# FC1 in 128 channels and two side-by-side halves of 64, and FC2's bias on POOL, in a shifted-window attention block

## The reference, cut to what matters

```python
f = residual + f.transpose(0, 3, 1, 2)
m = _ln(f.transpose(0, 2, 3, 1), g2, b2)
m = jax.nn.gelu(m @ w_fc1 + b_fc1, approximate=False) @ w_fc2 + b_fc2
return f + m.transpose(0, 3, 1, 2)
```

## Time and profile before

| | us |
|---|---|
| median of 3 runs (2 others: 3062.35, 3064.25) | 3063.34 |
| the profiled execution | 3062.91 |
| its span, first to last instruction | 3061.1 |
| TensorE busy (matmuls) | 2862.6 |
| VectorE, ScalarE, POOL busy | 2424.3, 2076.6, 1454.5 |

### The profile page before, as it was taken

How to read it: one execution, slowest core, us unless ns; L and a number is a source line. 1 busy time by engine, 2 the same in 40 slices (tenths; PEclk the granted TensorE clock), 3 DMA queues, 4 the chain that set the end, 5 groups by cost and what they waited for, 6 DMA issues and landing times.

```text
span 3061.1 us, 137479 instructions
## 1 busy us (share of the span) xinstructions
PE 2862.6 (94%) x53060; PEld 2299.2 (75%) x53060; DVE 2424.3 (79%) x7208; ACT 2076.6 (68%) x3208; POOL 1454.5 (48%) x1832
## 2 busy tenths in 40 slices
PE   1799999999999999999999999999999999999997
PEld 0677777777777777777777777777777777777775
DVE  5778888788887888788787888878888788888885
ACT  0467767667776767767766767767767667777674
POOL 2554454454444444444444454444454454445444
PEclk9899999999999999999999999999999999999999
DMA  1444444444444444444444444444444444444441
GB/s 29 108 119 123 124 125 119 119 126 122 126 127 113 123 123 122 126 121 120 124 126 114 125 124 120 124 123 120 123 125 118 120 126 121 126 127 119 125 113 42
DMA packets 414727, 359.37 MB, mean 117 GB/s; under 512 B 63455, under 2 KB 413985, under 8 KB 414012
## 3 DMA queue, kind: packets, MB, share of 16 engines
q1 hardware_dynamic: 414028, 350.01, 43.7%
HBM read 193.25 MB, written 154.14 MB: 113 GB/s over the span
## 4 chain that ended last, share of the span: by engine, by line
PE 87%; issue 5%; ACT 5%; DVE 2%; POOL 1%; SPq 0%; DMA 0%; POOLq 0%; DVEq 0%; ACTq 0%
PE psum L446 18%; PE psum L379 16%; PE psum L559 11%; PE psum L430 10%; PE psum L414 8%; PE psum L472 7%; PE psum L487 6%; PE psum L532 5%; ACT probs L618 4%; PE psum L522 3%; PE psum L395 2%; PE psum L511 1%; DVE st L754 1%; POOL rs L349 0%; DVE xfl L765 0%
## 5 line engine op out<-in xcount | busy, mean ns | idle before, releaser
L618 ACT ACTIVATE probs<-psum 113x784 f32<-113x784 f32 x768 | 633.2, 824 | 652.0 <-PE psum L430 648.9
L730 DVE TENSOR_REDUCE nmax<-psum 113x16 f32<-113x784 f32 x768 | 745.3, 970 | 153.9 <-PE psum L414 153.3
L342 POOL TENSOR_SCALAR ve<-mv 98x8 f32<-98x8 f32 x264 | 64.5, 244 | 1482.4 <-DVE mv L759 1476.5
L446 PE MATMUL psum<-vbd,probs 128*49 128x18 f32 x24576 | 644.2, 198 | 9.8 <-issue 9.0
L446 PEld LDWEIGHTS psum<-vbd,probs 128*49 128x49 f32 x24576 | 634.4, 126 | 14.1 <-issue 13.3
L349 POOL TENSOR_TENSOR rs<-ve,half 98x8 f32<-98x8 f32 x264 | 440.0, 1667 | 0.0
L430 PE MATMUL psum<-qbd,kst 128*49 128x196 f16 x6144 | 405.1, 251 | 36.3 <-DVE xfl L765 23.2
L754 DVE BATCH_NORM_STATS2 st<-tok 98x6 f32<-98x96 f32 x2112 | 363.6, 245 | 84.3 <-ACT tok L625 70.8
L354 POOL TENSOR_TENSOR xn<-xn,rs 98x768 f32<-98x768 f32 x264 | 388.4, 1471 | 72.7 <-POOL rs L349 72.7
L414 PE MATMUL psum<-kbd,qst 128*49 128x196 f16 x6144 | 401.4, 250 | 7.6 <-issue 4.2
L765 DVE TENSOR_TENSOR xfl<-psum,xfh 96x784 f16<-96x784 f32 x264 | 256.0, 970 | 176.0 <-ACT xfh L630 174.2
(11 more groups left out here) (83 smaller groups left out, 5270.1 us busy)
## 6 DMA issues: line engine op xcount, KB each, us to landing
stack_pages<-nat SPq DMA_DIRECT2D x256, 294.0 KB, 3.0
kst<-stack_pages SPq DMA_DIRECT2D x256, 220.5 KB
qbd<-stack_pages SPq DMA_DIRECT2D x1024, 55.1 KB
stack_pages<-nat SPq DMA_DIRECT2D x256, 147.0 KB, 2.0
xr<-in_x_dram SPq DMA_DIRECT2D x224, 147.0 KB, 3.4
out_dram<-yr SPq DMA_DIRECT2D x224, 147.0 KB, 2.2
qst<-stack_pages SPq DMA_DIRECT2D x256, 73.5 KB
kbd<-stack_pages SPq DMA_DIRECT2D x1024, 18.4 KB
```

Of the source, the lines that this page charges most:

```text
L446: last = nc.tensor.matmul(dst[:, :, h, :], probs[:, b.c % 2, h // 4, p, h % 4 * L:(h % 4 + 1) * L], vbd[:, b.c % 4, p * NH + h, :, :], sta ...
L618: nc.scalar.activation(probs[0:PR, b.c % 2, u, :, :].rearrange("j (g q) k -> j g (q k)", g=2), psum[0:PR, B:B + 2, 0:2 * CH], ACT.Exp).the ...
L730: nc.vector.tensor_reduce(dst, psum[0:PR, A:A + 2, 0:2 * CH].rearrange("i g (q h j) -> i g q h j", q=2, j=L), axis=AX.X, op=ALU.max, negat ...
```

## The change

FC1 now makes hidden channels 0 to 127 for all 392 tokens of a band with one group of three matmuls on the whole array (`most_and_rest`, first loop), written as two pieces of 196 tokens into the two halves of one bank. The remaining 64 channels (`REST`) are made for tokens 0 to 195 on partitions 0 to 63 and for tokens 196 to 391 on partitions 64 to 127 of the next bank, in turn, three pairs of matmuls over 196 columns. The Gelu reads these three pieces, 3 x 196 elements on 128 partitions, and `hid` has that shape. FC2 works on half a band (196 tokens) at a time: the first 128 hidden channels with `w2[:, 0]`, and the third piece with weights that are zero for the other half's 64 partitions (`w2[:, 1 + s]`). There is no free partition for the row of ones, so POOL adds FC2's bias to f before VectorE adds FC2 to it, with a semaphore `f_biased` that `result` waits for.

```diff
+PART = TOK // 2
+REST = HID - 128
+BIAS = -4
...
-        wp, w2 = sb("wp", [FULL, C]), sb("w2", [FULL, 2, C])
-        vec = sb("vec", [C, 5])
+        wp, w2 = sb("wp", [FULL, C]), sb("w2", [FULL, 3, C])
+        vec = sb("vec", [C, 6])
...
-        hid = sb("hid", [FULL, 2, 2, TOK])
+        hid = sb("hid", [FULL, 2, 3, PART])
...
+        def three_parts(bank):
+            return psum[:, bank:bank + 2, :].rearrange("p b (s r) -> p (b s) r", s=2)[:, 0:3, 0:PART]
...
+            const(w2[:, 0, :], wfc2[0:FULL, :])
             for m in range(2):
-                const(w2[0:C, m, :], wfc2[m * C:(m + 1) * C, :])
-            const(w2[C:C + 1, 0, :], bfc2.rearrange("(a c) -> a c", a=1))
+                const(w2[REST * m:REST * (m + 1), 1 + m, :], wfc2[FULL:HID, :])
...
+            def add_bias(b):
+                pool.wait_ge(t_made, b.step(AFTER).count(1, 1))
+                alone(pool)
+                nc.gpsimd.tensor_scalar(f[:, b.c % 8, :], f[:, b.c % 8, :], vec[:, BF:BF + 1], None, ALU.add).then_inc(f_biased, 1)
...
                 if has(t.step(ORDER)):
                     order_x(t.step(ORDER))
+                if has(t.step(BIAS)):
+                    add_bias(t.step(BIAS))
...
+            def most_and_rest(bank, high, low, b, kind):
+                products = ((high, xfh), (high, xfl), (low, xfh))
+                for n, (weights, tokens) in enumerate(products):
+                    nc.tensor.matmul(three_parts(bank)[:, 0:2, :], weights[:, 0:FULL], tokens[:, b.c % 4, kind, :].rearrange("c (s t) -> c s t", s=2),
+                                     start=n == 0, stop=n == 2)
+                for n, (weights, tokens) in enumerate(products):
+                    for s in range(2):
+                        last = nc.tensor.matmul(psum[REST * s:REST * (s + 1), bank + 1, 0:PART], weights[:, FULL:FULL + REST], tokens[:, b.c % 4, kind, s * PART:(s + 1) * PART],
+                                                start=n == 0, stop=n == 2)
+                return last
...
-                for m in range(2):
-                    last = three(psum[0:C, (B, A)[n] + m, 0:TOK], w1h[:, m * C:(m + 1) * C], w1l[:, m * C:(m + 1) * C], b, 1)
+                last = most_and_rest((B, A)[n], w1h, w1l, b, 1)
...
-                for m in range(2):
-                    last = nc.tensor.matmul(psum[0:C, D + n, 0:TOK], w2[:, m, :], hid[:, b.c % 2, m, :], start=m == 0, stop=m == 1)
+                for s in range(2):
+                    dst = psum[0:C, D + n, s * PART:(s + 1) * PART]
+                    nc.tensor.matmul(dst, w2[:, 0, :], hid[:, b.c % 2, s, :], start=True, stop=False)
+                    last = nc.tensor.matmul(dst, w2[:, 1 + s, :], hid[:, b.c % 2, 2, :], start=False, stop=True)
...
-                nc.scalar.activation(hid[0:C, b.c % 2, :, :], psum[0:C, at:at + 2, 0:TOK], ACT.Gelu, scale=1 / GAIN).then_inc(gelu_done, 1)
+                nc.scalar.activation(hid[:, b.c % 2, :, :], three_parts(at), ACT.Gelu, scale=1 / GAIN).then_inc(gelu_done, 1)
...
-            for a in (wide, wide1, wp, w2, xfh, xfl, oT, hid, kst, probs):
+            nc.vector.memset(w2[:, 1:3, :], 0.0)
+            for a in (wide, wide1, wp, xfh, xfl, oT, kst, probs):
...
-            nc.vector.memset(hid[C:C + 1, :, 0, :], 1.0).then_inc(rows_one, 1)
...
                 dve.wait_ge(fc2_made, b.count(1, 1))
+                dve.wait_ge(f_biased, b.count(1, 1))
```

More of the change, by code:

```diff
@@ L62 @@
 AFTER = 8
+BIAS = -4
 HIDDEN, RESULT, STORE = (-5, -4), (-6, -5), (-7, -6)
-N_CONST = 9 + 5 + 4 + 6
+N_CONST = 9 + 6 + 4 + 6
 class Band:
@@ L115, in build @@
         w1h, w1l = sb("w1h", [FULL, HID], F16), sb("w1l", [FULL, HID], F16)
-        wp, w2 = sb("wp", [FULL, C]), sb("w2", [FULL, 2, C])
-        vec = sb("vec", [C, 5])
-        G1, B1, BP, G2, B2 = range(5)
+        wp, w2 = sb("wp", [FULL, C]), sb("w2", [FULL, 3, C])
+        vec = sb("vec", [C, 6])
+        G1, B1, BP, G2, B2, BF = range(6)
         xr = sb("xr", [C, 4, WS, SIDE])
@@ L175, in build @@
         ot_made, o_in, proj_made, f_made = sem("ot_made"), sem("o_in"), sem("proj_made"), sem("f_made")
+        f_biased = sem("f_biased")
         fc1_made, gelu_done, fc2_made, y_made = sem("fc1_made"), sem("gelu_done"), sem("fc2_made"), sem("y_made")
@@ L229, in _ @@
             const(wp[0:C, :], wproj)
+            const(w2[:, 0, :], wfc2[0:FULL, :])
             for m in range(2):
-                const(w2[0:C, m, :], wfc2[m * C:(m + 1) * C, :])
-            const(w2[C:C + 1, 0, :], bfc2.rearrange("(a c) -> a c", a=1))
+                const(w2[REST * m:REST * (m + 1), 1 + m, :], wfc2[FULL:HID, :])
             const(brow[C:C + 1, :], bqkv.rearrange("(a c) -> a c", a=1))
             const(brow1[C:C + 1, :], bfc1.rearrange("(a c) -> a c", a=1))
-            for n, v in ((G1, g1), (B1, b1), (BP, bproj), (G2, g2), (B2, b2)):
+            for n, v in ((G1, g1), (B1, b1), (BP, bproj), (G2, g2), (B2, b2), (BF, bfc2)):
                 column(n, v)
@@ L701, in _ @@
             dve.wait_ge(filled, 1)
-            nc.vector.memset(xfh[C:C + 1, :, :, :], 1.0)
-            nc.vector.memset(hid[C:C + 1, :, 0, :], 1.0).then_inc(rows_one, 1)
+            nc.vector.memset(xfh[C:C + 1, :, :, :], 1.0).then_inc(rows_one, 1)
             nc.vector.memset(psum[:, :, :], 1.0).then_inc(psum_clear, 1)
```

## The result

The changed kernel took 3044.98 us (median of four runs, 3039.4 to 3049.6), the kernel before 3062.85 beside it: a ratio of 0.9942, 95% interval 0.9922 to 0.9963. It is faster, by 17.9 us and not by 42. In a second set of runs it was 0.9931 (0.9914 to 0.9948). The forecast of 3021 and the range from 3000 to 3034 were wrong.

A forecast was written before the change was run, and what follows sets the result against it. TensorE, busy 94% of the span, was taken as the bound, waiting for the second Gelu ahead of the transposes. From 3062.9 us, 128 x 0.34 = 43.5 saved, FC2 +3 and start -1 gave 3021; range 3000 to 3034.

The forecast's parts named there:

- The steady pair: One ordinary pair of steps: transposes start 0.34 us sooner, FC2 costs 0.024 more, pairs 0.32 us shorter.
- the switches: FC1 on TensorE: changing between whole array and halves costs 0.12 us in and 0.10 out, 0.34 in FC1.
- the halves: FC1's 64-channel matmuls over 196 columns run side by side: 0.085 us a pair, six pairs 0.51.
- rival 1: FC1's halves don't run side by side at 64 channels: FC1 2.34 us, kernel 3084 us; chance 0.06.
- rival 4: Gelu on ScalarE keeps its 0.82 us: only 0.18 us a pair, 23 us, kernel 3042; chance 0.06.
- rival 3: TensorE's mode changes in FC1 cost nothing: 0.50 us a pair sooner, 64 us, kernel 3001; chance 0.08.
- rival 2: Weight loads of short matmuls lie open: in FC2 up to +1.31 us a pair, kernel 3187; chance 0.03.
- about 0.3: Sign expected in the changed profile: TensorE's wait ahead of the transposes, 0.47 us before, at about 0.3.
- 3010: Fast end of the forecast's own range, 3010 to 3032, taken from a gain of 0.45 us a pair.
- POOL's add: FC2's bias added on POOL once a band: 0.6 us, at the upper end 1.5, delaying nobody.
- The sum: Whole kernel: 3062.9 - 43.5 + 3 - 1 = 3021.4 us, with 0.34 us gained in each of 128 pairs.
- 0.02 for an unseen wait: Chance 0.02 that a wait not seen takes the whole gain back, leaving the time within 0.2%.

The follow-up runs named there:

- the last experiment: Changed kernel with loop written out, back transposes waiting for the first Gelu alone, FC1 ordered wide, halves, halves, wide: 2937.19 us, 0.9604 of the kernel before.
- 200 more: Changed kernel with 200 semaphore increments added at the head of TensorE's program, ahead of the loop: 0.9852 of the kernel before.

## Why the prediction was wrong

- **The steady pair** was right. FC1 1.85, measured 1.87; the switches 0.12 and 0.10; the halves 0.085 a pair (0.083 in the last experiment), so they do run side by side at 64 channels (rival 1 out: three pairs one after the other would take 0.49 and all six halves took 0.37); Gelu 0.655, measured 0.660, on the path only once (rival 4 out); the switches are paid (rival 3 out); FC2's loads stay hidden, +0.02 (rival 2 out); nobody waits for POOL. Forecast 0.32 a pair shorter net, measured 0.29. The wait ahead of the transposes is 0.21; the prediction's "about 0.3" does not follow from its own times, which give 0.16 (1517.81 less 1517.65), nor does its 3010, since 0.45 a pair gives 3007.
- **POOL's add** took 1.27 us, not 0.6. That was inside the bound of 1.5, and POOL's wait of 5.6 us took it.
- **The sum failed** where it multiplied 0.34 by all 128 pairs, 43.5 us, and stopped. Six of the pairs hold a branch, and what the change adds to TensorE's program had no term but its own time. These six were forecast 2 us shorter together and came out 17 us longer in the profiled execution (157.0 to 174.1), because behind the branch TensorE stopped for its program inside L422 and then ran 3.4 to 10.2 us at half clock behind five of them. By the kernels with the loop written out the term is 15 to 20 us. With it, 3021 becomes 3036 to 3041; the median was 3045. The rest lies in the 118 ordinary intervals, 7 us short of the forecast: half of it is 0.29 for 0.32 a pair, half more time above the commonest length. The rows were there to be seen: the longest pairs of before, 25.0 to 26.8 us, were never looked at, since all rows came from one ordinary pair.
- The **0.02 for an unseen wait** was the only place for this, and it stood for the whole gain. Every instruction that the change added on TensorE, ahead of the loop or in it, moved all that follow in its program, the body's start by 56; the bounds should have taken in the dearest branch pair of before against the cheapest, some 2 us, at six places, and more for half clock.
- **What stays open.** That the stop is TensorE waiting for its program rests on its place, on the packets' times and on the reaction to padding; the views themselves name no releaser. Why the stop comes in some executions and not in others at the same place is not shown (six, then three of six branches of one kernel), nor whether the stop brings on the long half clock that mostly follows it, since three long stretches came with no stop near them, nor why 200 more has 11 stops in its whole profile where the kernel before, whose body starts at the same place, has 28.

## What to carry to other kernels

Before multiplying a steady period by its count, list the length of every period and explain the longest ones; loops cost at their branches, and an edit that adds instructions can change that cost by more than its own. When a small change in a looped kernel measures oddly, pad the busiest engine's program or write the loop out before believing or rejecting the idea behind it. And read what a long wait really protects: here its semaphore count was one Gelu too high.

## What the runs showed of the hardware

- Idle instructions ahead of a loop, with no work of their own, moved the time of one and the same loop by 0.8% (0.9931 to 0.9852 of before with none and with 200).
- All 440 stops inside groups of equal matmuls, in 14 profiles, end 1.21 to 1.71 us after a packet of the instruction queue q8; behind a branch the first place for one is after 26, 37 or 51 matmuls, by where the body starts, and the next 124 matmuls on.
- Switching the array between whole and halves cost 0.12 in and 0.10 out beside matmuls of 196 and 392 columns; beside the attention's groups it was 0.12 in and 0.14 out, ahead of transposes.
- A weight load of 128 fp16 channels has a shorter record than one of 96: 98 ns against 123. The Trainium skill's page "TensorE: Matmul & The Clock Gate", section "Weight-path perf modes", states a faster load for exactly 128 weights that are not fp32; the rows agree that it is faster.
